# A Mamba scan in a decoder layer: the decay's exponential is left in its PSUM bank, and VectorE's product carries it to SBUF

## The reference

```
def step(h, inp):
    dA_t, dt_t, B_t, C_t, x_t = inp
    h = h * dA_t[..., None, None] + (dt_t[..., None] * x_t)[..., None] * B_t[:, None, None, :]
    y_t = jnp.einsum('bhpn,bn->bhp', h, C_t)
    return (h, y_t)
```

## Time and profile before

| | |
|---|---|
| Time of three executions | 4574.5, 4575.61 (median), 4576.97 us |
| Span of the profiled execution | 4575.4 us |
| Median less span | 0.2 us |
| Busy in the span: PE, DVE, ACT, POOL | 4119.9, 3193.2, 1655.0, 1006.2 us |

### The profile page before, as it was taken

The page is one execution under the profiler, slowest core; times in us unless marked ns, Lnnn a source line. Parts: engine busy times, 40 slices in busy tenths (PEclk is TensorE's granted clock), DMA queues, the critical chain, the costliest instruction groups (busy, mean ns, idle before and its releaser), DMA issues. The chain is left out here.

```text
span 4575.4 us, 72562 instructions
## 1 busy us (share of the span) xinstructions
PE 4119.9 (90%) x26456; PEld 3062.0 (67%) x26456; DVE 3193.2 (70%) x6928; ACT 1655.0 (36%) x3487; POOL 1006.2 (22%) x597
## 2 busy tenths in 40 slices
PE   6999999997898989889858888888898799999999
PEld 5776767664666666666547666666576577778777
DVE  5888888875588888887765746647646576666664
ACT  3333334332333333333325726627446321111111
POOL 1333333333144444444510000000000100000000
PEclk9999999998899999999979999999999899999999
DMA  2110111102001101101034143243242210000000
GB/s 104 36 41 24 40 37 41 38 22 102 17 30 45 43 32 50 43 32 43 30 141 118 48 139 105 64 143 93 70 144 67 91 60 28 28 28 31 28 31 19
DMA packets 144918, 265.90 MB, mean 58 GB/s; under 512 B 25140, under 2 KB 31288, under 8 KB 144568
## 3 DMA queue, kind: packets, MB, share of 16 engines
q1 hardware_dynamic: 144568, 261.27, 17.2%
HBM read 164.58 MB, written 88.08 MB: 55 GB/s over the span
## 5 line engine op out<-in xcount | busy, mean ns | idle before, releaser
L1774 DVE TENSOR_REDUCE xa_mn<-xa_s 128x1 f32<-128x896 f32 (+7 forms) x512 | 373.4, 752 | 135.6 <-PE xa_s L1869 134.5
L1689 ACT ACTIVATE xa_src<-xa_s,xa_mn 128x896 f32<-128x896 f32 (+7 forms) x512 | 378.2, 741 | 229.7 <-DVE xa_mn L1774 228.3
L1875 PE MATMUL xa_gen<-xa_ident,xa_src 128*128 128x128 f32 x2304 | 310.6, 278 | 53.2 <-ACT xa_pT L1698 26.2
L72 PE MATMUL ff_wb<-ff_w_hi,ff_st_hi 128*128 128x512 f32 x768 | 323.1, 421 | 10.1 <-DVE ff_parts L2380 10.1
L1636 POOL TENSOR_TENSOR xa_res<-xa_res,xa_bor 128x512 f32<-128x512 f32 x32 | 40.8, 1280 | 1248.2 <-DMA xa_res<-after_mamba_dram 1248.2
L73 PE MATMUL ff_wb<-ff_w_hi,ff_st_lo 128*128 128x512 f32 x768 | 310.2, 404 | 0.0
L74 PE MATMUL ff_wb<-ff_w_lo,ff_st_hi 128*128 128x512 f32 x768 | 309.6, 403 | 0.0
L1875 PEld LDWEIGHTS xa_gen<-xa_ident,xa_src 128*128 128x128 f32 x2304 | 251.5, 143 | 75.1 <-ACT xa_src L1689 59.6
L1217 PE MATMUL mb_ib<-mb_wc,mb_yT 128*128 128x512 f32 x512 | 267.8, 672 | 1.8 <-DVE mb_y L988 1.0
L2148 POOL TENSOR_TENSOR ff_mixed<-ff_at,ff_rw 128x1024 f32<-128x1024 f32 x32 | 61.0, 1906 | 872.2 <-DVE ff_at L2408 872.2
L1217 PE MATMUL mf_ib<-mf_wc,mf_yT 128*128 128x512 f32 x512 | 248.1, 630 | 1.8 <-DVE mf_y L988 1.0
(11 more groups left out here) (514 smaller groups left out, 11421.6 us busy)
## 6 DMA issues: line engine op xcount, KB each, us to landing
xa_qa<-xa_q_dram SPq DMA_DIRECT2D x384, 64.0 KB, 2.0
xa_q_dram<-xa_kq SPq DMA_DIRECT2D x32, 512.0 KB, 2.8
xa_k_dram<-xa_kq SPq DMA_DIRECT2D x32, 512.0 KB, 2.8
xa_ka<-xa_k_dram SPq DMA_DIRECT2D x192, 64.0 KB, 2.0
xa_st<-xa_k_dram SPq DMA_DIRECT2D x192, 64.0 KB, 2.0
mf_xg<-in_x_dram SPq DMA_DIRECT2D x16, 512.0 KB, 5.3
turned_dram<-mf_xt_hi SPq DMA_DIRECT2D x16, 512.0 KB, 2.6
turned_dram<-mf_xt_lo SPq DMA_DIRECT2D x16, 512.0 KB, 3.9
```

The costliest lines, as they stand in the source:

```text
L72: nc.tensor.matmul(out, w_hi, x_hi, start=first, stop=False)
L1689: a_.activation(pq[:, hh, 0:w], s1[g, i, hh][:, 0:w], ACT.Exp, scale=-1.0, bias=mn[:, i % 2, hh:hh + 1], accum_out=sums[:, i // QT, i % QT ...
L1774: v_.tensor_reduce(mn[:, i % 2, hh:hh + 1], s1[g, i, hh][:, 0:(i + 1) * P], AX.X, ALU.min).then_inc(mx_ready.sem, 1)
L1875: last = tr(ps[:, n * P:(n + 1) * P], pq[:, hh, j * P:(j + 1) * P], ident[:])
```

## The change

The exponential is written back into its own PSUM bank; the product reads that bank and writes to `decay`. ScalarE no longer waits for the readers of `decay` (`intra_full`), VectorE does instead, and a bank is handed back to TensorE by the product (`mix_ready`) where it was handed back by the exponential (`exp_ready`).

```diff
                 if n + 2 < N:
-                    dec += [(("d", n + 2, q), exp_ready, NQ * (n + 2) + q) for q in range(NQ)]
+                    dec += [(("d", n + 2, q), mix_ready, NQ * (n + 2) + q) for q in range(NQ)]
...
                 for q in range(NQ):
                     wait(act, d_full, NQ * c + q)
-                    wait(act, intra_full, NQ * c + q - ER)
-                    a_.activation(decay[:, (NQ * c + q) % ER], dec["d", c, q][:].rearrange("p (h n) -> p h n", h=Q4), ACT.Exp)\
-                        .then_inc(exp_ready.sem, 1)
+                    a_.activation(dec["d", c, q][:], dec["d", c, q][:], ACT.Exp).then_inc(exp_ready.sem, 1)
...
                     for q in range(NQ):
                         wait(dve, exp_ready, NQ * c + q)
-                        d = decay[:, (NQ * c + q) % ER]
-                        v_.tensor_tensor(d, d, bcast(gb[:, c % 2, 0:P], 1, Q4), ALU.mult).then_inc(mix_ready.sem, 1)
+                        wait(dve, intra_full, NQ * c + q - ER)
+                        v_.tensor_tensor(decay[:, (NQ * c + q) % ER], dec["d", c, q][:].rearrange("p (h n) -> p h n", h=Q4),
+                                         bcast(gb[:, c % 2, 0:P], 1, Q4), ALU.mult).then_inc(mix_ready.sem, 1)
```

## The result

The changed kernel takes 4662.6 us (median of four executions, 4658.07 to 4666.19) beside 4576.24 us for the kernel before: 1.019 times as long, interval 1.0178 to 1.0202, 86 us more. The forecast was 4670 us.

A forecast was written before the change was run, and what follows sets the result against it. The prediction took PE to bound the forward pass, and VectorE to bound backward where PE waits for L988. 64 + 35 + 7 - 12 = 94 us on 4575.6 gave 4670 us (chance 0.60), range 4625 to 4730 (0.90).

The forecast's parts named there:

- The exponential into PSUM, zero: ScalarE's exponential, PSUM to PSUM: any difference of a few tenths is hidden behind four projection matmuls; taken as zero.
- The product, 0.68 us, none at 2 us: VectorE's product reading a bank: mean near 684 ns in both passes, none at 2 us, no longer held by GpSimd.
- The small steps inherit the waits for GpSimd: L228 and the like between products still meet GpSimd; gain only 0.9 us per steady odd chunk backward, 12 us.
- the faster rival: Small steps don't inherit the GpSimd waits and new PE waits are hidden: backward gains up to 64 us, 4512 us; chance 0.06.
- The bank's late return forward, 64 us: Forward, the second mask matmul of pair 1 waits for VectorE's product: 54 us in 13 odd chunks, 10 us in others.
- chunk of the first kind: Seven forward odd chunks with 4.7 us later mask matmuls; six of the second kind, product sooner relative to PE, 3.5 us.
- The clock, 35 us: Forward, matmuls behind the new PE holes run at a lower granted clock: 2.9 us in seven chunks, 2.2 in six, 1.7 once.
- the rival without the clock: Slower, but the forward holes leave the clock alone: 4670 - 35 = 4635 us; chance 0.13.
- Backward, -12 and +7: Backward: 12 us gained in 13 steady odd chunks, 20 us of new waits vanish at L988, 7 us stay in three other chunks.
- The rival in which backward pays too: Backward, VectorE has to wait for the convolution's channels: 12 us lost, 20 of waits and 20 of clock added, 4722 us; chance 0.17.
- the forecast's sum of 94 us: Whole kernel: 64 forward waits + 35 clock + 7 backward waits - 12 backward gain, 2.1% slower.

The follow-up runs named there:

- the release alone: Kernel before with only the decay bank's release moved from exponential to product; exponential still to SBUF, product in place there: 4771.23 us, 1.0423 times before.
- the early products: Changed kernel with VectorE's first two products of a chunk moved, forward only, to right behind the closing of the state: 4609.39 us, 1.0071 times before.
- the filled hole: Changed kernel with matmuls that no output needs added ahead of the second pair of mask matmuls in 13 forward odd chunks: 4645.15 us, 1.0146 times before.
- the last experiments: Kernel with the change backward alone: first two exponentials before residual's activation, 4568.44 us; also two products before the sum, 4569.02; exponentials' move on kernel before, 4574.13.
- The same early place: Changed kernel, first two products behind the closing of the state in both passes, backward first pair's exponentials ahead of residual's activation: 4627.01 us, 1.0096 times before.
- the third product early: Changed kernel, forward only: first two products behind the closing of the state, third right behind the sum of outputs: 4569.35 us, 0.9984 times before.

## Why the prediction was right, point by point

**The exponential into PSUM, zero.** Right: 580 and 575 ns, 15 to 17 less than into SBUF. ScalarE has over 170 us of idle time before it in each pass.

**The product, 0.68 us, none at 2 us.** Right: 685 ns in both passes, 685 to 687 in every kernel that reads PSUM. The 65 ns more for a PSUM source, an estimate from the Trainium skill's cycles (page "VectorE: DVE Perf Modes", section "The TRN2 errata — SBUF-src ops pay a fixed extra latency per instruction") are not seen: an undisturbed product from SBUF took 0.68 us as well.

**The small steps inherit the waits for GpSimd.** Right in kind, but small: backward L231's mean went from 425 to 651 ns, and in the chunk shown it stands until L637 ends. All small steps together (L221 to L234) take 12.6 us more backward (L231 21.7 more, L234 9.9 more, L228 18.8 less) and 6.8 less forward, where the products lost 63 and 69. So this is not what kept the faster rival away. In the steady chunks backward VectorE is busy 66.0 us less (753.7 to 687.7), and most of that became idle time, since the freed time of the even chunks lies where TensorE is the bound.

**The bank's late return forward, 64 us.** Right in place and cause, which the release alone and the early products show from both sides. Per chunk of the first kind the second half of the projection moved by 9.79 - 4.50 = 5.29 us (forecast 4.7), of the second by 8.03 - 4.48 = 3.55 (3.5). With 7 and 6 such chunks that is 58.3 us where the sum had 54; all 13 taken singly give 58.6.

**The clock, 35 us.** Right in kind, too large. The second half of the projection lost 2.21 to 2.85 us behind the longer wait and 1.70 behind the shorter, once 2.47 (forecast 2.9 and 2.2): 28.1 us in the 13 chunks where the sum had 34. I took the 2.9 from a hole in another place. The wait in the third chunk from last, 1.51 us, left the clock alone (3.70 us), and some old losses went: in four even chunks the second half began 6.19 us behind the first before and begins 4.68 behind it now. Part of what the clock costs also stands in the 5.29, as the mask matmuls and sums between run slower too. The two terms together, 58.6 + 28.1 = 86.7 us in the 13 chunks, meet the forecast's 54 + 34 = 88; the filled hole bears out that the clock is a part of it (20 us less, with 3 us of added work), against the rival without the clock. That the whole forward pass comes as close is in part luck: the first two chunks cost 10.7 us where I had 6.7, and the even ones from chunk 4 on gave 3.5 us back where I had them pay.

**Backward, -12 and +7.** The sign was right, the mechanism only in part. The steady chunks, from the start of the first mask matmul of chunk 3 to that of chunk 29 in the two timelines: 923.1 us (1300.80 to 2223.89) became 902.4 (1405.11 to 2307.49), 20.7 us less, where I took 12 for VectorE alone. VectorE's relief is there. In the odd chunk shown it needed 6.33 us from the first product's start to the fourth's end (1688.65 to 1694.98); before, the fourth product stood here, and so ended 7.92 us behind the first's start:

```profile
1597.91 0.69 DVE L1027 TENSOR_TENSOR mb_decay<-mb_decay,mb_gb 128x512 f32<-128x512 f32 x1
```

But only 4.7 us of the 20.7 came in the stretches from odd to even, which end with TensorE waiting for VectorE. Nine of these 13 got shorter, by 0.6 to 1.4 us; in four the new waits were not swallowed, and they grew by 5.5 us in all. The other 16.0 us came from even to odd, where TensorE is the bound and its clock rose. To that the forecast gave nothing: it priced the clock behind the new holes forward and not what a shorter old hole would give back. Outside the steady chunks 20.7 - 14.6 = 6.1 us stayed (forecast 7), but by luck: 8.1 us came in ahead of them, and 2.0 us went behind them, where I had 4.8 and 2.3 more. That the new waits vanish in the old one is shown: 36.3 us of them came and 41.7 us of "issue" went, and the last experiments moved idle time between the two. The rival in which backward pays too falls, as the pass got shorter.

So the forecast's sum of 94 us is above the 82.5 us between the two profiled executions by two errors of one direction: forward 96 us for 64 + 35 = 99, backward -14.6 for -5, the gain 10 us too small since its larger part, the clock, was left out.

## What to carry to other kernels

When a buffer's release moves from an early reader to a later one, look first at where in its own list the new reader stands relative to the engine that wants the buffer back, and follow every next user of the ring: with two products moved up the stall only went to the third bank's next user, with three it was gone. The same early place was free forward and cost 20 us backward, where it put TensorE's idle time back ahead of a stretch that TensorE bounds, so such a move is judged pass by pass. And a stall of the matrix engine is to be priced with what stands behind it: here 1.7 to 2.9 us of slow matmuls on top of 2.7 to 4.0 us of waiting where TensorE was the bound, and in nine of 13 stretches backward nothing, where it had to wait for VectorE soon after. A change that moves a stall from the first kind of place to the second gains, even if the idle time stays.

## What the runs showed of the hardware that was not expected

A short hole can do to the clock what a long one does. In the run with two early products forward the new holes before the product of B and C are 0.7 us in seven odd chunks and 1.1 us in three (the other two of the 12 lie in the first two chunks), against the 2.7 to 4.0 us that they replaced. Behind each of the seven the clock fell to 0.50 2.5 to 3 us later; behind the three longer ones it did not, so the length of the hole alone does not decide, and what does is not shown. The mean granted clock from 1 to 1104 us stayed at 0.94, as in the changed kernel, while it was 0.97 both with the holes filled and with the third product early. Two windows of the run with two early products, the first behind the hole of 0.71 us shown above, which ended at 345.90 (PEclk is the third number from the end):

```profile
349.00:352.00 3.00, 3.00 (x16) 3.00 (x16) 0.94 (x4) 1.20 (x2) 2.92 (x2) 0.50 0.39 137
1.00:1104.00 1103.00, 1018.88 (x5479) 744.87 (x5511) 763.95 (x1936) 406.33 (x814) 329.42 (x179) 0.94 0.11 40
```

ScalarE's exponential is faster into its PSUM bank than into SBUF, 580 and 575 ns for 595 and 592. The Trainium skill, page "ScalarE: Activation LUTs", section "Step-by-step: what each stage is for", says that PSUM is the faster destination for ScalarE; the trace agrees, with some 15 ns on a 128x512 tile.
